# A ranking network's lookups, pair products and tower: pair rows along diagonals in three chunks, weights loaded later

## The reference

```python
e = jnp.stack([tbl_0[ids[:, 0]], ..., tbl_26[ids[:, 26]]], axis=1)        # (512, 27, 128)
interactions = jnp.einsum('bnd,bmd->bnm', e, e)
i, j = jnp.triu_indices(27, k=1)
z = interactions[:, i, j]                                                # (512, 351)
h = jnp.concatenate([z, dense_ctx], axis=1)                              # (512, 367)
h = jnp.maximum(h @ W_top1 + b_top1, 0.0)                                # (367, 512)
h = jnp.maximum(h @ W_top2 + b_top2, 0.0)                                # (512, 256)
y = h @ W_top3                                                           # (256, 1)
```

## Time and profile before

| | |
|---|---|
| time, median of 3 runs | 112.94 us (112.81 to 113.18) |
| profiled execution, first to last instruction | 141.2 us |
| its mean granted TensorE clock | 0.891 |
| TensorE matmul busy | 112.1 us (79%), 1025 records |
| VectorE, ScalarE, GpSimd busy | 73.8, 70.5, 68.8 us |
| DMA | 15,877 packets, 18.74 MB |

### The profile page before, as it was taken

How to read it: one execution, slowest core, us unless ns; L and a number is a source line. 1 busy time by engine, 2 the same in 40 slices (tenths; PEclk the granted TensorE clock), 3 DMA queues, 4 the chain that set the end, 5 groups by cost and what they waited for, 6 DMA issues and landing times.

```text
span 141.2 us, 2513 instructions
## 1 busy us (share of the span) xinstructions
PE 112.1 (79%) x1025; PEld 93.6 (66%) x1025; DVE 73.8 (52%) x68; ACT 70.5 (50%) x100; POOL 68.8 (49%) x81
## 2 busy tenths in 40 slices
PE   5969999998999987069994212126999999999894
PEld 5938777775877865047892110105999998899792
DVE  2799999999999980699100000200446212451221
ACT  4099999999999960699440000002255211151021
POOL 2578788887877887147877777740000000002000
PEclk9999999999999999965899555555599999999999
DMA  2896788989768699201112222110037543004300
GB/s 62 292 357 220 239 241 268 267 252 279 170 229 258 150 383 331 61 0 37 48 45 56 60 56 56 44 49 0 14 119 188 118 105 49 0 5 143 54 0 1
DMA packets 15877, 18.74 MB, mean 133 GB/s; under 512 B 9425, under 2 KB 11805, under 8 KB 15738
## 3 DMA queue, kind: packets, MB, share of 16 engines
q1 hardware_dynamic: 11864, 13.39, 32.1%
q0 software_dynamic: 2000, 4.06, 10.2%
q10 hardware_dynamic: 2002, 1.14, 2.8%
HBM read 16.80 MB, written 1.77 MB: 132 GB/s over the span
## 4 chain that ended last, share of the span: by engine, by line
PE 42%; DVE 31%; issue 18%; another core or an unknown queue 4%; DMA 3%; SPq 0%; ACT 0%; DVEq 0%
DVE hot L500 22%; PE psG L386 14%; DVE parts L505 9%; PE psG L369 7%; PE psG L413 5%; PE psH L398 5%; PE psH L429 4%; DMA pick_ids<-in_picked_ids 3%; PE psT L347 3%; PE psG L429 1%; PE psH L444 1%; DVE hot L488 1%; PE psG L444 0%; SPq L264 0%
## 5 line engine op out<-in xcount | busy, mean ns | idle before, releaser
L328 POOL DMA_INDIRECT rows<-in_tbl,ids_sb x61 | 62.9, 1032 | 19.7 <-issue 15.8
L369 PE MATMUL psG<-hot,parts 128*128 128x512 f32 (+1 forms) x216 | 56.1, 410 | 7.7 <-DVE hot L500 6.2
L369 PEld LDWEIGHTS psG<-hot,parts 128*128 128x128 f32 x216 | 40.7, 198 | 19.9 <-DVE hot L500 6.2
L500 DVE TENSOR_TENSOR hot<-pick_ids,psH 128x1536 fp32r<-128x1536 int32 (+2 forms) x23 | 41.6, 1851 | 5.3 <-remote 5.3
L386 PE MATMUL psG<-ET 128*52 128x54 f32 x512 | 20.2, 234 | 17.3 <-issue 17.3
L386 PEld LDWEIGHTS psG<-ET 128*52 128x52 f32 x512 | 17.5, 146 | 20.3 <-issue 19.7
L513 DVE COPY gram<-psG 128x432 f32<-128x432 f32 x8 | 7.2, 903 | 36.0 <-issue 21.3
L597 ACT COPY gram<-psG 128x432 f32<-128x432 f32 x8 | 7.2, 905 | 32.0 <-remote 23.2
L586 ACT ACTIVATE hot<-pick_ids,row_no 128x512 fp32r<-128x512 int32 (+1 forms) x30 | 19.4, 711 | 0.0
L210 POOL DMA_DIRECT2D zT<-pair_blocks x1 | 0.9, 883 | 35.9 <-DMA pair_blocks<-gram 35.9
L505 DVE TENSOR_TENSOR parts<-table,parts 128x1024 fp32r<-128x1024 f32 (+1 forms) x12 | 16.3, 1358 | 0.0
(11 more groups left out here) (35 smaller groups left out, 47.0 us busy)
## 6 DMA issues: line engine op xcount, KB each, us to landing
table<-in_tbl SPq DMA_DIRECT2D x6, 640.0 KB
table<-in_tbl SPq DMA_DIRECT2D x6, 512.0 KB
pick_ids<-in_picked_ids SPq DMA_DIRECT2D x11, 256.0 KB, 3.3
w_sb<-in_w SPq DMA_DIRECT2D x1, 1024.0 KB
rows<-in_tbl,ids_sb POOLq DMA_INDIRECT x61
pair_blocks<-gram ACTq DMA_DIRECT2D x4, 144.0 KB, 2.5
pair_blocks<-gram SPq DMA_DIRECT2D x4, 144.0 KB, 3.5
w_sb<-in_w SPq DMA_DIRECT2D x1, 512.0 KB
```

The source lines that it names most:

```text
L328: pool.indirect_dma_start(out=rows[:, n % RING, x, :], out_offset=None, in_=gathered_tables[f], in_offset=bass.IndirectOffsetOnAxis(ap=ids ...
L369: last = pe.matmul(psP[:, k % 2, 0:looked_up(k)], parts[:, k % 2, x, c, :], hot[:, k % 2, c, 0:looked_up(k)], start=x == 0 and c == 0, sto ...
L500: dve.tensor_tensor(hot[:, k % 2, first:end, 0:many], pick_ids[:, k % TABLES, 0:many].unsqueeze(1).to_broadcast(shape), numbers.unsqueeze( ...
```

## The change

The gram of a tile is now written by one DMA from SP and one from ScalarE, whole (27 x 32 floats for each partition, one run), and not in two column blocks. Seen as one list of 729 positions i * 27 + j, every seventh position from 1, 2 or 3 on holds pairs with j - i equal to 1, 2 or 3 modulo 7, each unordered pair once; the pairs with a difference of 7 or 14 modulo 28 are every 28th position from 7 (26 of them) and from 14 (13). So a chunk is 104 rows with step 7 and 13 rows with step 28, two DMAs, and three chunks of 117 rows hold the 351 pairs with none left over. The 16 dense rows are split over chunks 0 and 1. The product matmuls take all 54 columns as weights in place of 52. For the last tile SP, ScalarE and GpSimd read one chunk each. `w1` has three chunks. `w1` and `w2` are issued by SP behind a wait for the one-hot columns of all 12 tables, and the dense rows (two DMAs) and the small inputs right behind the third table.

```diff
@@ -47,13 +47,13 @@
-    J = F - 1
-    NB = F // WIDTH
-    PAIR_ROWS = [sum(WIDTH * (end - first) for b, first, end in chunk) for chunk in CHUNKS]
-    ROWS = PAIR_ROWS[:NC - 1] + [PAIR_ROWS[NC - 1] + DN]
+    PAIR_ROWS = [sum(end - first for step, offset, first, end in chunk) for chunk in CHUNKS]
+    DENSE_IN = 2
+    DH = DN // DENSE_IN
+    ROWS = [n + (DH if c < DENSE_IN else 0) for c, n in enumerate(PAIR_ROWS)]
@@ -72,8 +72,9 @@
-    SP_READS = [(0, 1, 2), (0, 1, 2, 3), (0, 1, 2, 3), (0, 2)]
-    ACT_READS = [(3,), (), (), (1,)]
+    SP_READS = [(0, 1), (0, 1, 2), (0, 1, 2), (0,)]
+    ACT_READS = [(2,), (), (), (1,)]
+    POOL_READS = (2,)
@@ -132,7 +133,7 @@
-        blocks = nc.dram_tensor("pair_blocks", (T, NB, S, G, WIDTH * GH), fp32, kind="Internal").ap()
+        grams = nc.dram_tensor("pair_grams", (T, S, G, F * GH), fp32, kind="Internal").ap()
@@ -177,38 +177,24 @@
-        def write_last_block(eng, t, s):
-            eng.dma_start(blocks[t, NB - 1, s, :, :],
-                          gram[s:P:S, t % 2, s, WIDTH * (NB - 1):F, :].rearrange("q j g -> q (j g)")
-                          ).then_inc(last_block_out[t], 16)
-        def write_other_blocks(eng, t, s):
-            src = gram[s:P:S, t % 2, s, 0:WIDTH * (NB - 1), :]
-            eng.dma_start(blocks[t, 0:NB - 1, s, :, :].rearrange("b q x -> q b x"),
-                          src.rearrange("q (b j) g -> q b (j g)", b=NB - 1)).then_inc(other_blocks_out[t], 16)
+        def write_gram(eng, t, s):
+            eng.dma_start(grams[t, s, :, :], gram[s:P:S, t % 2, s, :, :].rearrange("q j g -> q (j g)")
+                          ).then_inc(gram_out[t], 16)
         def read_pairs(eng, t, c):
             r = 0
-            for b, first, end in CHUNKS[c]:
-                n = WIDTH * (end - first)
-                src = blocks[t, b, :, :, :].rearrange("s (h i) x -> (s h) i x", h=H)[:, first:end, :]
+            for step, offset, first, end in CHUNKS[c]:
+                n = end - first
+                src = grams[t, :, :, :].rearrange("s (h i) x -> (s h) (i x)", h=H)
+                src = src[:, 0:step * GH * end].rearrange("q (m k g) -> k m q g", k=step, g=GH)
                 eng.dma_start(zT[r:r + n, t, c, :].rearrange("r (q g) -> r q g", q=Q),
-                              src.rearrange("q i (j g) -> (i j) q g", g=GH)).then_inc(chunk_in[t][c], 16)
+                              src[offset, first:end, :, :]).then_inc(chunk_in[t][c], 16)
                 r += n
@@ -275,22 +261,23 @@
+                if k == TABLES - 1:
+                    for c in range(DENSE_IN):
+                        sp.dma_start(zT[PAIR_ROWS[c]:ROWS[c], :, c, :],
+                                     dense_rows[DH * c:DH * (c + 1), :].rearrange("k (t p) -> k t p", p=P)).then_inc(dense_in, 16)
+                    sp.dma_start(b1_sb[:, :], b1_cols).then_inc(small_in, 16)
+                    sp.dma_start(b2_sb[:, :], b2_cols).then_inc(small_in, 16)
+                    sp.dma_start(w3_sb[:, :], w3_cols).then_inc(small_in, 16)
+            sp.wait_ge(hot_ready, 2 * FP)
             sp.dma_start(w1_sb[:, :, :], w1_chunks).then_inc(w1_in, 16)
-            sp.dma_start(zT[PAIR_ROWS[NC - 1]:ROWS[NC - 1], :, NC - 1, :],
-                         dense_rows.rearrange("k (t p) -> k t p", p=P)).then_inc(dense_in, 16)
             sp.dma_start(w2_sb[:, :, :], w2.rearrange("(k p) n -> p k n", p=P)).then_inc(w2_in, 16)
-            sp.dma_start(b1_sb[:, :], b1_cols).then_inc(small_in, 16)
-            sp.dma_start(b2_sb[:, :], b2_cols).then_inc(small_in, 16)
-            sp.dma_start(w3_sb[:, :], w3_cols).then_inc(small_in, 16)
             for t in range(T):
                 sp.wait_ge(gram_dve, U * (t + 1))
                 sp.wait_ge(gram_act, U * (t + 1))
-                write_last_block(sp, t, 0)
-                write_other_blocks(sp, t, 0)
+                write_gram(sp, t, 0)
+                wait_written(sp, t)
                 for c in SP_READS[t]:
-                    wait_block_of(sp, t, c)
                     read_pairs(sp, t, c)
@@ -333,8 +320,9 @@
-            wait_block_of(pool, T - 1, 3)
-            read_pairs(pool, T - 1, 3)
+            wait_written(pool, T - 1)
+            for c in POOL_READS:
+                read_pairs(pool, T - 1, c)
@@ -383,8 +371,8 @@
-                            last = pe.matmul(psG[R * h:R * h + S * J, m % 2, bank, S * F * x:S * F * (x + 1)],
-                                             group[:, 0:S * J], group, start=True, stop=True)
+                            last = pe.matmul(psG[R * h:R * h + S * F, m % 2, bank, S * F * x:S * F * (x + 1)],
+                                             group, group, start=True, stop=True)
@@ -660,17 +647,17 @@
-WIDTH = 9
-CHUNKS = [[(2, 0, 14)], [(1, 0, 14)], [(0, 0, 8), (1, 14, 17)], [(2, 14, 26)]]
+CHUNKS = [[(7, 1, 0, 104), (28, 7, 0, 13)], [(7, 2, 0, 104), (28, 7, 13, 26)], [(7, 3, 0, 104), (28, 14, 0, 13)]]
```

More of the change, by code:

```diff
@@ L166, in dlrm_tower @@
         gram_act = sem("gram_act")
-        last_block_out = [sem(f"last_block_out_{t}") for t in range(T)]
-        other_blocks_out = [sem(f"other_blocks_out_{t}") for t in range(T)]
+        gram_out = [sem(f"gram_out_{t}") for t in range(T)]
         chunk_in = [[sem(f"chunk_in_{t}_{c}") for c in range(NC)] for t in range(T)]
@@ L178, in dlrm_tower @@
         out_done = sem("out_done")
-        def write_last_block(eng, t, s):
-            eng.dma_start(blocks[t, NB - 1, s, :, :],
-                          gram[s:P:S, t % 2, s, WIDTH * (NB - 1):F, :].rearrange("q j g -> q (j g)")
-                          ).then_inc(last_block_out[t], 16)
-        def write_other_blocks(eng, t, s):
-            src = gram[s:P:S, t % 2, s, 0:WIDTH * (NB - 1), :]
-            eng.dma_start(blocks[t, 0:NB - 1, s, :, :].rearrange("b q x -> q b x"),
-                          src.rearrange("q (b j) g -> q b (j g)", b=NB - 1)).then_inc(other_blocks_out[t], 16)
[L192 to L197, removed]
+        def write_gram(eng, t, s):
+            eng.dma_start(grams[t, s, :, :], gram[s:P:S, t % 2, s, :, :].rearrange("q j g -> q (j g)")
+                          ).then_inc(gram_out[t], 16)
         def wait_written(eng, t):
-            eng.wait_ge(last_block_out[t], 16 * S)
-            eng.wait_ge(other_blocks_out[t], 16 * S)
+            eng.wait_ge(gram_out[t], 16 * S)
         def read_pairs(eng, t, c):
             r = 0
-            for b, first, end in CHUNKS[c]:
-                n = WIDTH * (end - first)
-                src = blocks[t, b, :, :, :].rearrange("s (h i) x -> (s h) i x", h=H)[:, first:end, :]
+            for step, offset, first, end in CHUNKS[c]:
+                n = end - first
+                src = grams[t, :, :, :].rearrange("s (h i) x -> (s h) (i x)", h=H)
+                src = src[:, 0:step * GH * end].rearrange("q (m k g) -> k m q g", k=step, g=GH)
                 eng.dma_start(zT[r:r + n, t, c, :].rearrange("r (q g) -> r q g", q=Q),
-                              src.rearrange("q i (j g) -> (i j) q g", g=GH)).then_inc(chunk_in[t][c], 16)
+                              src[offset, first:end, :, :]).then_inc(chunk_in[t][c], 16)
                 r += n
@@ L257, in dlrm_tower @@
         steps += mlp(2) + [("read", T - 1), ("layer3", T - 2), ("chunk", 0), ("chunk", 1), ("chunk", 2),
-                           ("chunk", 3), ("relu1", T - 1), ("layer2", T - 1), ("layer3", T - 1)]
+                           ("relu1", T - 1), ("layer2", T - 1), ("layer3", T - 1)]
         block = ctx.enter_context(nc.Block())
@@ L407, in layer1_chunk @@
                     pe.wait_ge(w1_in, 16)
-                    pe.wait_ge(dense_in, 16)
+                    pe.wait_ge(dense_in, 16 * DENSE_IN)
                 pe.wait_ge(chunk_in[t][c], 16 * len(CHUNKS[c]))
@@ L601, in write_half @@
                 act.wait_ge(gram_act, U * (t + 1))
-                write_last_block(act, t, 1)
-                write_other_blocks(act, t, 1)
+                write_gram(act, t, 1)
             def read_half(t):
+                wait_written(act, t)
                 for c in ACT_READS[t]:
-                    wait_block_of(act, t, c)
                     read_pairs(act, t, c)
@@ L662, in pair @@
         a, b = sorted((features[i], features[j]))
[L663 to L667, removed]
+        return a * n - a * (a + 1) // 2 + b - a - 1
+    chunks = [[pair(*divmod(step * m + offset, n)) for step, offset, first, end in chunk for m in range(first, end)]
+              for chunk in CHUNKS]
+    for c in range(2):
+        chunks[c] += [n * (n - 1) // 2 + x for x in range(n_dense // 2 * c, n_dense // 2 * (c + 1))]
     return [c + [-1] * (128 - len(c)) for c in chunks]
 PICKED = 12
-WIDTH = 9
-CHUNKS = [[(2, 0, 14)], [(1, 0, 14)], [(0, 0, 8), (1, 14, 17)], [(2, 14, 26)]]
+CHUNKS = [[(7, 1, 0, 104), (28, 7, 0, 13)], [(7, 2, 0, 104), (28, 7, 13, 26)], [(7, 3, 0, 104), (28, 14, 0, 13)]]
 def kernel(**inputs):
```

## The result

| | time, median | one profiled execution: span; start of its last tile's first unit; end of the last copy |
|---|---|---|
| before | 112.95 us (13 runs) | 111.1; 92.43; 109.51 (run f1_before_undisturbed, below) |
| after | 111.53 us (13 runs) | 109.6; 92.21; 108.00 |

The ratio is 0.9847, with a 95% interval of 0.9816 to 0.9879: 1.7 us of 112.95 (1.4 to 2.1 by the interval), where 1.7 was forecast. Every ratio here compares only the fast runs, those within 1.5% of the kernel's fastest, which can be few, so where it matters the medians of all runs stand beside it. Those of the 13 runs of each kernel are 1.42 us apart. The time of an execution is its span and about 2 us around it (113.24 and 111.1 before, 111.63 and 109.6 after), not the 3.5 that I had put around a span computed too short.

A forecast was written before the change was run, and what follows sets the result against it. TensorE bounds the tail; before it the gathers end last, nearly tied with TensorE. Tail saving 1.88 us, less 0.1 for wider weights and 0.1 waiting, gives 1.7: 112.94 - 1.7 = 111.2 us, range 109.6 to 112.6.

The forecast's parts named there:

- the 3.5 that I had put around a span: Whole execution: median 3.5 us above the computed undisturbed span of 109.4 us, kept fixed.
- the prediction's own signs: Wrong if chunks open near 1 us late, last gather has landed when TensorE comes, or clock falls in last tile.
- The tail, 1.9 forecast less 0.2: Last tile's first unit to end: layer 1 of tile 2 and last tile save 0.94 us each; 0.1 twice comes off.
- The units: Product matmuls with 54 weight columns for 52: 0 to 0.12 us more over the tail's 128 records, taken as 0.1.
- the mis-sized term: TensorE ahead of the last tile's chunks: 0.1 us of waiting altogether, 0.4 to 1.4 with a late write.
- Tiles 0 and 1, 1.9 us saved and 0 counted: Ahead of quads 14 and 15: shorter layer 1 saves 1.9 us, worth 0 if the gathers end last.
- The gathers' estimate: Before the last tile: last gather lands at 94.4 to 95.5, about 1.2 us of work follow, unit at 95.6 to 96.7.
- Rival A: Before the last tile: TensorE's chain, not the gathers, ends last; time 109.3 to 110.4 us; 15 in 100.
- The write and reads: Last tile's gram: one write done at 129.6 for 130.2, every read waiting for all, 0.4 us later than before.
- The loads, cost 0: Lookup stage: weights behind the last one-hot columns and small inputs behind the third table cost 0 and gain 0.
- Rival D: Lookup stage: weight loads cost timed runs up to 3.5 us, which goes; time 107.7 to 110.5 us; 5 in 100.
- Rival C: Last gather: TensorE waits 2.4 us instead of 0.5, clock falls, 2.8 us lost; time 114.0 us; 8 in 100.

The follow-up runs named there:

- f1_before_undisturbed: The kernel before, unchanged, profiled again on a chip without the two disturbances: span 111.1 us, 112.94 us in 17 timed runs.
- filler: Changed kernel plus 8 matmuls of the identity ahead of layer 1 of tile 0: 0.985 of before (0.9775 to 0.9925), profiled span 108.6 us.
- disturbed trace: First profiled execution of the unchanged kernel before, with VectorE idle 5.30 us and TensorE slowed: span 141.2 us against a timed median of 112.94.
- chunks-only kernel: Kernel before with three chunks and single writes, loads where they were: 0.9819 (111.42 us) on an undisturbed chip, 0.9852 (143.59 us) on a starved one.
- identity: Changed kernel, layer 1 of tiles 0 and 1 multiplying the identity without waiting for chunks, those outputs wrong: 0.9806 of before, median 110.79 us.

## Why the prediction was right, step by step

The time, 111.53 us, lies in the range of 109.6 to 112.6, and the gain comes from the tail, as forecast. In the middle the number, 0, was right and the reason was not: by the prediction's own signs it was wrong there, since the last gather had landed when TensorE came to it.

**The tail, 1.9 forecast less 0.2.** From the last tile's first unit to the start of the last copy it was 16.80 us, again 16.80 in the undisturbed trace, and 15.51 after: 1.29 shorter, where I had 1.7. By parts: layer 1 of tile 2 and of the last tile each went from 3.84 to 2.94 or 2.95 us, 0.90 each for my 0.94. The units went from 3.32 to 3.41 us, 0.09 for my 0.1. The rest is the mis-sized term, the waiting for the last tile's chunks, 0.33 us for my 0.1. The write was all in 2.7 us after its issue (2.6 forecast), so SP's read went out at 99.46; chunk 0 came 2.6 us after that, within my 2.15 to 3.25 but above the 2.5 that a wait of 0.1 us allows. The Trainium skill (DMA: Bandwidth & Descriptors, Anatomy of one DMA) made it 2.1 us after the second of the two issues, 99.8, and so 101.9: the chunk came 0.2 later. That section's formula is for DMAs that GpSimd issues, which the prediction did not say of its estimate for a read by SyncE; GpSimd's own two reads here, 52 and 6.5 KB, landed in 2.5 and 2.0 us. They never held TensorE up. In all six traces of undisturbed three-chunk kernels the wait for chunk 0 is 0.17 to 0.33 us and the tail 1.3 to 1.45 us shorter than before.

**Tiles 0 and 1, 1.9 us saved and 0 counted.** That is what came. The last tile's first unit starts at 92.21 after and at 92.43 before, but the whole of that was there before the pair stage: the first product unit started at 65.25 and at 65.62. From the one to the other it is 26.81 and 27.36 us in the two four-chunk traces, and 26.96, 27.13, 27.15, 27.29 and 27.36 in the five with three chunks and no filler. The saved matmuls became waits. So the traces show 1.3 to 1.45 us, which fits the medians (1.42) and lies at the low end of the ratio's 1.4 to 2.1. That the ratio gives just the 1.7 forecast is luck within its interval.

**But the reason was wrong.** I had TensorE at this unit at 95.6 and the gathers at 95.6 to 96.7 in the disturbed trace's time, 90.3 and 90.3 to 91.4 without the 5.30 us. The gathers' estimate held: in three traces the last one landed at 89.8 to 90.2, and 1.2 us of work bring that to at most 91.4. TensorE's was short by 2.1 us. It missed the wait for tile 0's and tile 1's gram to go out to memory and come back, 1.3 us before and up to 3.5 with three chunks. In the disturbed trace tile 0's write went out 1.4 us ahead of quad 10's transposes, and by the time that TensorE wanted the chunk, 7.6 us later, it was there. Undisturbed the write goes out 0.4 us ahead (70.06 and 70.44), and the chunk came 8.1 us behind it. SP's four read issues alone took 3.71 us for 1.85 (1.75 to 3.37 in the three-chunk traces). The gathers were running then and not in the disturbed trace; that they are the cause is not shown, as no run has it apart. The rows of the disturbed trace:

```profile
101.09 0.53 SPq L182 DMA_DIRECT2D pair_blocks<-gram  x1
...
104.84 1.85 SPq L210 DMA_DIRECT2D zT<-pair_blocks  x4
```

So TensorE's chain ends last in seven of the eight undisturbed traces, by 0.9 to 1.4 us in the three that have the landing. The gather ends last in one, where it landed 1 us later than in those. Rival A was therefore true in its order and false in its price, since the saved work didn't come through the waits. One thing of the forecast stands: the last gather is close behind, and is the next to stop TensorE.

**The write and reads.** One write for two: right within 0.1 us in the tail. In the middle tile 0's two writes, issued together, are in 3.0 to 5.1 us later in the six traces, and all readers now wait for the whole of them; tile 2's copies waited for all of it before as well. This is where the three-chunk traces differ most from one another.

**The loads, cost 0.** Wrong by 0.5 us (1.0047, interval above 1). Rival D, that they disturb the lookups, is refuted: on the starved chips the idle time stayed where they had gone, and in the undisturbed trace with the loads in place there is none.

**The clock.** Rival C named the mechanism and missed the place. The gap that let the clock fall is the one ahead of tile 0, not the one at quad 15. It cost 1.70 us on 24 records, of which 0.84 reached the last tile: with the filler a wait for tile 1's chunk took the rest. The Trainium skill (TensorE: Matmul & The Clock Gate, HAM oscillation) describes such falls behind waits for a DMA that are longer than these. Here gaps of 1.91, 1.96 and 2.06 us were followed by a fall, and so was one of 1.31 in the chunks-only kernel on a starved chip. One of 1.33 before was not, nor was one of 2.32 in the chunks-only kernel. What decides is open. The runs show how often: a mean clock of 0.985 or less in three of 47 undisturbed runs with four chunks, and in 13 of 37 with three chunks and neither filler nor identity.

**What stays open**: which of the moved loads costs, why taking the reads off GpSimd is slower, and what starves TensorE on some chips.

## What to carry to other kernels

Count saved work only in the stretch whose end it sets: here 3.7 us of matmuls were taken away, 1.8 in the tail, where 1.3 to 1.45 came through, and 1.9 in the middle, where TensorE waited for a round trip through memory and nothing came through that the traces show. Compare such a stretch from its own start: the executions already differed by 0.4 us when it began. Take a transfer's time from rows beside the traffic that it will have; a trace in which other work had stalled gave too short a round trip, and hid the wait that bounds the middle. A queue that waits for a DMA before it issues the next holds up every copy behind it, as ScalarE's did for 4.04 us. Putting the copies that another engine waits for ahead of reads that can wait shortened the waits in one trace; that it saves time is not shown.

## What the runs showed of the hardware

On two chips TensorE sat idle for nothing that the profile shows in the first product units, with its clock at the 0.5 level for 20 us and more, and the time was 27 to 29% longer (medians of 143.18 and 145.5 us for 112.95), in all kernels and all runs there. The two 216 KB writes of a tile, issued together, were in after 2.7 us in the tail and after 3.0 to 5.1 beside gathers, though all DMA together moved about as much (153 to 180 GB/s for 158). Four read issues of SyncE took 1.75 to 3.71 us beside gathers, and 1.85 in the trace without. The clock can fall after an idle gap of 1.9 us and can hold through one of 2.3; of two gaps of 1.3 us, on two chips, one was followed by a fall and one was not.
